# Sixty one-column matmuls dealt between the parts of a key product, and later transposes and ranks dealt between key and value products

## The reference, cut to what matters

```python
xn = _layernorm(x)
x = x + gnn(xn, edges) + linear_attention(xn)   # two graph-attention layers; keys and values of all rows
x = x + ffn(_layernorm(x))                      # eight experts, two for each row, and a shared one
# linear_attention:
q = elu(q) + 1;  k = elu(k) + 1
kv = einsum('bhsd,bhse->bhde', k, v)            # out = q @ kv, normalised, then w_proj
```

## Time and profile before

| | |
|---|---|
| device time, 3 runs | 1650.14 us median (1647.8 to 1651.68) |
| the profiled execution | 1642.05 us, of it 1640.0 us span |
| TensorE busy | 95% of the span |
| VectorE, ScalarE, GpSimd busy | 49%, 20%, 15% |
| first stage, until GpSimd's first scatter | 81.5 us |
| scatters | from 81.5 to 221.2 us |

### The profile page before, as it was taken

One profiled execution on the slowest core, in us unless ns is written; L12 is line 12 of the kernel. 1 busy time (PEld: TensorE's weight loads), 2 busy tenths in 40 slices (PEclk: granted clock), 3 DMA queues, 4 the chain that ended last, 5 costly groups with the idle time before them and its releaser, 6 DMA issues.

```text
span 1640.0 us, 21951 instructions
## 1 busy us (share of the span) xinstructions
PE 1555.6 (95%) x8501; PEld 1034.3 (63%) x8502; DVE 811.2 (49%) x1539; ACT 335.1 (20%) x493; POOL 250.7 (15%) x234
## 2 busy tenths in 40 slices
PE   6999999999899999998989999999999999999995
PEld 4466666557779999998987555444444444444442
DVE  7545447998867899984887433111111111111111
ACT  2321112001223255560372110100100000001000
POOL 1087820000000000000000027111111111111111
PEclk9999999999999999999979999999999999999998
DMA  9900020000004536213111318925629211613415
GB/s 268 339 2 1 2 61 1 1 1 1 1 1 117 160 80 187 58 26 84 32 46 59 144 44 170 327 63 197 221 52 323 92 48 53 211 42 122 136 30 193
DMA packets 85337, 163.79 MB, mean 100 GB/s; under 512 B 18874, under 2 KB 48816, under 8 KB 85001
## 3 DMA queue, kind: packets, MB, share of 16 engines
q1 hardware_dynamic: 66903, 119.07, 22.6%
q0 software_dynamic: 12096, 23.27, 6.3%
q10 hardware_dynamic: 6258, 20.40, 4.6%
HBM read 127.75 MB, written 37.56 MB: 101 GB/s over the span
## 4 chain that ended last, share of the span: by engine, by line
PE 62%; DVE 11%; POOL 8%; DMA 7%; issue 6%; SPq 3%; ACT 1%; DVEq 1%; ACTq 0%; POOLq 0%
PE bank L803 28%; POOL slot_table L1312 7%; PE bank L1629 6%; PE bank L1667 5%; PE bank L1531 5%; PE bank L1588 3%; PE bank L713 2%; DVE arena L2388 2%; PE bank L1467 2%; SPq L372 2%; DVE arena L2357 2%; PE bank L1414 2%; PE bank L1715 1%; DMA arena<-out_dram,arena 1%; DVE arena L2333 1%
## 5 line engine op out<-in xcount | busy, mean ns | idle before, releaser
L803 PE MATMUL bank<-arena 128*64 128x384 f32 x3312 | 540.7, 488 | 2.3 <-DMA arena<-in_L_ffn_w_down_dram 1.7
L803 PEld LDWEIGHTS bank<-arena 128*64 128x64 f32 x3312 | 237.1, 137 | 294.2 <-issue 291.4
L1156 DVE SCALAR_TENSOR_TENSOR arena<-bank,arena 64x384 f32<-64x384 f32 x88 | 50.3, 610 | 355.2 <-DMA arena<-out_dram,arena 214.4
L1667 PE MATMUL bank<-arena 125*125 125x198 f32 (+1 forms) x1200 | 193.9, 323 | 11.0 <-DVE arena L2357 10.8
L1667 PEld LDWEIGHTS bank<-arena 125*125 125x125 f32 x1200 | 187.3, 198 | 15.5 <-DVE arena L2357 15.2
L1629 PE MATMUL bank<-arena 128*125 128x192 f32 x960 | 163.7, 328 | 4.7 <-DVE arena L2310 3.8
L1629 PEld LDWEIGHTS bank<-arena 128*125 128x125 f32 x960 | 157.6, 189 | 5.5 <-DVE arena L2310 4.1
L1312 POOL DMA_INDIRECT slot_table<-arena x80 | 110.1, 1376 | 104.5 <-issue 104.5
L2194 DVE TENSOR_TENSOR arena<-arena,bank 125x417 f32 x186 | 109.4, 588 | 27.2 <-PE bank L1467 18.9
L2388 DVE SCALAR_TENSOR_TENSOR arena<-arena 125x1250 f32<-125x1250 f32 x60 | 90.8, 1514 | 10.6 <-ACT arena L1904 10.6
L664 POOL MEMSET arena<- 1x2500 f32 x1 | 2.2, 2177 | 598.3 <-DVE arena L2340 598.3
(11 more groups left out here) (307 smaller groups left out, 1528.2 us busy)
## 6 DMA issues: line engine op xcount, KB each, us to landing
arena<-in_L_ffn_w_gate_dram SPq DMA_DIRECT2D x9, 2304.0 KB, 9.3
arena<-in_L_ffn_w_up_dram SPq DMA_DIRECT2D x9, 2304.0 KB, 10.6
arena<-in_L_ffn_w_down_dram SPq DMA_DIRECT2D x9, 2304.0 KB
arena<-score_rows ACTq DMA_DIRECT2D x18, 585.9 KB
expert_in<-arena SPq DMA_DIRECT2D x23, 384.0 KB, 9.6
arena<-expert_in ACTq DMA_DIRECT2D x23, 384.0 KB, 6.0
arena<-in_L_mix_w_qkv_dram SPq DMA_DIRECT2D x2, 2304.0 KB, 17.7
xn_columns<-arena SPq DMA_DIRECT2D x1, 3750.0 KB, 15.0
```

What stands on the lines that cost most here:

```text
L803: ins = tp.matmul(ps[bank][HP * h:HP * h + HP, 0:384], frm[:, b, k, HP * h:HP * h + HP], ew[h][i][:, k, n * 384:(n + 1) * 384], start=(k = ...
L1667: ins = tp.matmul(ps[bank][0:T, c * width:(c + 1) * width], ptile[0:T, j % NPT, dt * T:(dt + 1) * T], values(n - first, st), start=(st == ...
```

## The change

In the totals the two matmuls of a bucket now stand next to each other, and the buckets come in KD = 6 groups of five: `edge_totals(k)` issues ten matmuls behind the k-th matmul of `key_product(1, 0)`. The semaphores are the same; `s_kps` is given by the last matmul of the product, ahead of the last ten small ones. `turn_x(4)` and `turn_x(5)` move ahead of `key_product(2, 1)`, `turn_x(6)` and `(7)` stay behind it, `edge_work(1)` follows, and `turn_x(8)` and `(9)` come behind that. ScalarE's `take_x(4)` and `(5)` move ahead of `key_exp(2, 1)` in the same way. No operation is added or removed.

```diff
-            def edge_totals():
-                pe.wait_ge(s_oh, 5)
-                for b in range(NBK):
+            def edge_totals(k):
+
+                n = NBK // KD
+                if k == 0:
+                    pe.wait_ge(s_oh, 5)
+                for b in range(n * k, n * k + n):
                     tp.matmul(ps[4][:, b:b + 1], onehot[0:T, 0:P, b], ones_b[0:T, 0:1], start=True, stop=True)
-                for b in range(NBK):
                     ins = tp.matmul(ps[5][0:EC1, b:b + 1], onehot[0:T, P:EC, b], ones_b[0:T, 0:1], start=True, stop=True)
-                ins.then_inc(s_tot, 1)
+                if k == KD - 1:
+                    ins.then_inc(s_tot, 1)
...
-            def key_product(t, hf):
+            def key_product(t, hf, totals=False):
...
-                ins.then_inc(s_kps, 1)
+                    if k == KD - 1:
+                        ins.then_inc(s_kps, 1)
+                    if totals:
+                        edge_totals(k)
...
             key_product(0, 0)
-            key_product(1, 0)
-            edge_totals()
+            key_product(1, 0, totals=True)
             turn_x(2)
...
             key_product(1, 1)
+            turn_x(4)
+            turn_x(5)
             key_product(2, 1)
-            for t in range(4, NT):
-                turn_x(t)
+            turn_x(6)
+            turn_x(7)
             edge_work(1)
+            turn_x(8)
+            turn_x(9)
             pe.wait_ge(s_xta, XA)
...
             key_exp(1, 1)
+            take_x(4)
+            take_x(5)
             key_exp(2, 1)
-            for t in range(4, NT):
+            for t in range(6, NT):
                 take_x(t)
```

## The result

The changed kernel takes 1653.49 us (median of 20 runs, 1648.78 to 1661.77), the kernel before 1646.72 us (20 runs, 1641.53 to 1651.68): a ratio of 1.0044 with a 95% interval of 1.0032 to 1.0055. It is slower by about 7 us, the way that was forecast; 1653.49 lies in the range of 1650 to 1664. The profiled execution has a span of 1650.4 us (1640.0 before).

A forecast was written before the change was run, and what follows sets the result against it. The last rank leaving TensorE, then GpSimd's scatters, was taken to bound the kernel. Width changes 5.9, clock 2.8 and transposes 0.2 summed to +8.9 us: 1659.0 us against a median of 1650.14; own range 1655.2 to 1663.7, whole range 1650 to 1664.

The forecast's parts named there:

- What bounds the kernel: When the last rank leaves TensorE decides; GpSimd's 80 scatters follow, so each microsecond ahead of it moves the end equally.
- The price of a change of width: Totals between key matmuls: 30 round trips between wide and narrow weight tiles at 0.30 us each, 9.0 us.
- the forecast +5.9: Totals at full clock: 9.0 us of width changes plus 0.5 for key matmuls, less today's 3.6; bounds +3.5 to +6.8.
- The clock, +2.8: TensorE's clock falls at about the same time as before, making three of six parts 0.95 us longer each; bounds 0 to +6.3.
- Behind the totals ... I take 0: Transposes and key product behind the totals pay the low clock as today; product could save 1.4 or pay 2.5 more.
- The moved transposes, +0.2: Six transpose tiles in the new order, up to the first value product: 7.19 us against 6.97, +0.2 us.
- The margin of 0.4 us: VectorE's normalised rows are ready at 44.97, TensorE reaches tile 4 at 45.4, so no wait; without it, bound +0.5.
- The 0.08: Semaphore time added to the 0.74 us wait for the last copy ahead of the first value product, 0.82 together.
- the second rival: Width changes are paid but key matmuls between hold the clock at 1.00: +4.1, 1654.2 us, low price 1651.8; chance 18%.
- Hidden small matmuls: First rival: weight loads run ahead during key matmuls, small ones hide, clock stays up: -3.9, 1646.2 us; chance 12%.
- Clock held in spite of the changes: The second rival's claim: key matmuls between the small ones keep TensorE's clock at 1.00; +4.1 us, chance 18%.
- low bound of 0.22 for a round trip: Lowest price of one change of weight width there and back in the totals: 0.13 + 0.09 us.

The follow-up runs named there:

- E5: Kernel before, nothing spread, but the 60 small matmuls in one piece alternate 128 and 32 weight columns; ratio 1.0015 to the kernel before.
- E3: Changed kernel, but in each group of ten the five 128-column matmuls stand first, the five 32-column ones behind; ratio 1.0003 to the kernel before.
- E4: Changed kernel, but the second matmul of each bucket also loads 128 weight columns, so no change of width; ratio 1.0000 to the kernel before.
- E1: Kernel before with only the totals spread as in the change; transposes, ranks and copies in the old order; ratio 1.0057 to the kernel before.
- E7: Changed kernel with all small matmuls 128 columns wide, transposes as before, memory cleared behind GpSimd's constants; ratio 0.9997 to the kernel before.
- E8: Changed kernel, but thirty wide matmuls behind the first three key matmuls, thirty narrow behind the last three, transposes as before; ratio 0.9990 to the kernel before.
- E9: Kernel before plus 60 unread one-column matmuls ahead of the totals (20 wide, 20 narrow, ten alternating pairs), weights side by side; executed once, 1650.83 us.
- E6: Kernel before, nothing spread, with the second matmul of each bucket loading 128 columns, memory cleared behind GpSimd's constants; ratio 1.0014 to the kernel before.
- E11: Kernel before with the one-hot array stored bucket by bucket, so totals weights lie side by side; ratio 1.0101 to the kernel before.
- E12: Changed kernel with the one-hot array stored bucket by bucket, so the alternating pairs' weights lie side by side; ratio 1.0185 to the kernel before.
- E10: Kernel before with only the wide small matmuls spread, five behind each key matmul, narrow ones in one piece behind the product; ratio 1.0002 to the kernel before.

## Why the prediction was right, point by point

- **What bounds the kernel: right.** Last rank +10.07 us (76.99 to 87.06 for the start of its last matmul), first scatter +10.07, last scatter +10.08 (220.02 to 230.10), span +10.4; TensorE's line 1490 (line 1481 before) came behind its wait of 1.71 us for VectorE at 238.84, 10.06 later than 228.78.
- **The price of a change of width, "9.0 us" for the sixty: right.** 0.15 us a matmul, within 0.01 at both clocks, and 9.0 us in E5. Shown by taking the changes away (E3, E4) and by making them alone (E5). The Trainium skill says in "TensorEngine Tiling (Array Packing)", Key Properties, that a change of tiling mode drains the array. The runs agree in so far as each change of width costs 0.08 to 0.09 us; that a change of width is such a change of mode isn't shown. The Trainium skill says in "TensorE: Matmul & The Clock Gate", Part 2, that the next weights load while a matmul runs. Of the ten loads behind a long matmul the trace of E4 shows that for one. The size of the whole term was a little high: at full clock six parts would take 2.10 + 5 x 2.20 = 13.1 us: +5.5 against the forecast +5.9, because the first change of each group costs 0.10 and not 0.15.
- **The clock, +2.8: right in sum, by luck, and wrong in both factors.** I had three parts at +0.95. There were four at +0.73 (2.93 less 2.20), 2.9 us, so two errors cancelled. The clock fell sooner than I took it to, 4.4 us behind the first record of the product and not 6.6 (27.2 less 22.83, against 27.8 less 21.2). And a part at half clock cost less: the key matmuls doubled, while the small ones kept 0.15, the lower end of what I had allowed.
- **"Behind the totals ... I take 0": close.** The transposes took 2.97 us as before, the key product 5.12 instead of 5.39: -0.3.
- **The moved transposes, +0.2: right.** From the end of `key_product(1, 1)` to the first value product the changed kernel takes 55.13 to 68.86 = 13.73 us, E1 13.51, the kernel before 13.50. The margin of 0.4 us ahead of VectorE's rows held for the first tile and had gone for the second (0.79, with VectorE last), at no more cost than the queue behind `key_exp`. The 0.08 that the sum has for the semaphore ahead of the value product stood in no row; here it was 0.05 (copy done at 68.81, product at 68.86).
- **The sum:** 5.5 + 2.9 - 0.3 + 0.2 = 8.3, measured 8.4 from the product to the first scatter, forecast 8.9. The median moved by 6.8 us and the ratio says 7.2 (5.3 to 9.1).
- **The number for the whole kernel: 5.5 us too high, and in the range by its breadth.** The forecast was 1659.0, measured were 1653.49. Of the 5.5 us, 3.4 come from the median of three runs that it was added to (1650.14, where twenty runs give 1646.72), and 2.1 from the change itself. 1653.49 lies below the forecast's own range, 1655.2 to 1663.7, and nearest to the second rival's 1654.2; only the low end that the second rival gave the whole range takes it in. With 1646.72 the own range would have been 1651.8 to 1660.3, with the measured time in it. By the number alone the second rival fits best; what refutes it is the clock in the trace.
- **The rivals.** Hidden small matmuls: refuted by the changed trace, and by E4, where even without changes only one of each ten is quick. Clock held in spite of the changes: refuted by the windows; it is what happens when the changes go (E3, E4, E7, E8).
- **What was wrong** without touching the sum: half of the low bound of 0.22 for a round trip (its 0.09) came from a place whose weights lie side by side. E9 shows that weights side by side have another price, 0.22 a round trip (2 x 0.11), where it is 0.30 here.

## What to carry to other kernels

Before small matmuls are dealt between long ones, look at the widths of the weight tiles in the order that comes out. Each step between a wide and a narrow tile cost 0.08 to 0.09 us here, more than the small matmul itself, and sorting by width within each group, one line of code, took back 9.3 us where 8.4 had been lost. What spreading does give is the clock, some 2 us here (E6 against E7); that is a gain only if the spreading costs nothing else.

## What was not expected of the hardware

- The pace of a one-column matmul follows the places of its weights: 0.025 us for 128 or 32 columns side by side, 0.06 for both when they lie 60 bytes apart (E9, E11). Why 32 scattered columns cost as much as 128 stays open.
- At half clock neither the small matmuls (0.06: three steps in 28.44 to 28.62) nor the alternating ones (0.15) got slower; only those with many columns did. With weights side by side the alternating ones went from 0.11 (E9) to 0.12 (E12).
- GpSimd's clearing of memory held up VectorE. In E6 VectorE's cast of `dst` takes as long as the clearing beside it, 2.48 us. In E4 the clearing is over when the same cast (there line 1966) begins, and it takes 0.47:

```profile
5.25 2.50 POOL L1302 MEMSET arena<- 125x2880 bf16 x1
5.44 2.48 DVE L1956 CAST arena<-arena 125x320 f32<-125x320 int32 x1 [5.44 <-DMA arena<-in_dst_dram]
...
5.42 0.47 DVE L1966 CAST arena<-arena 125x320 f32<-125x320 int32 x1 [5.42 <-DMA arena<-in_dst_dram]
```

The cast ends 0.17 us behind GpSimd's clearing in E6 and in E7 too (7.92 behind 7.75, 7.94 behind 7.77). Not all of the delay is the clearing's: the transfer of `dst` landed 0.7 to 0.8 us later in both than before (5.44 and 5.29 against 4.62). At 0.47 us the cast of E6 would have ended at 5.91, so the clearing is worth 2.0 us.

- From the first transpose to `key_product(1, 0)` the same code took 6.8 to 8.4 us over these executions (21.33 less 14.51 in E10, 21.15 less 14.13 before, 22.83 less 14.78 after, 23.02 less 14.64 in E5), depending on when in it the clock rose: at 17.6 us before, at 20.3 after. That is a microsecond or more between executions that no edit made.
